# Masked cross-attention in a two-block transformer kernel: a new order of loads in SP's queue, reciprocals of 16 sums instead of 256 columns, masks made by VectorE, and a third buffer of last products

## The reference, cut to what matters

```
q = split_heads(layernorm(x) @ Wq + bq)          # 16 heads of 16
k = split_heads(ctx @ Wk + bk)                   # 257 keys per sequence
v = split_heads(ctx @ Wv + bv)
scores = einsum('bhqd,bhkd->bhqk', q, k) / 4
scores = where(mask[:, None] > 0, -1e9, scores)  # mask: 128 x 32 x 257, int32
p = softmax(scores)
x = x + einsum('bhqk,bhkd->bhqd', p, v) @ Wo + bo
```

## Time and profile before

| | |
|---|---|
| median of 3 runs | 3450.29 us (3443.96 to 3454.62) |
| profiled execution, its own time | 3441.18 us |
| its span in the profile | 3439.3 us |
| mean granted TensorE clock over the span | 0.879 |
| busy over the span | PE 78%, DVE 63%, ACT 54%, POOL 51% |
| HBM traffic over the span | 45 GB/s |

### The profile page before, as it was taken

The page is one execution under the profiler, slowest core; times in us unless marked ns, Lnnn a source line. Parts: engine busy times, 40 slices in busy tenths (PEclk is TensorE's granted clock), DMA queues, the critical chain, the costliest instruction groups (busy, mean ns, idle before and its releaser), DMA issues. The chain is left out here.

```text
span 3439.3 us, 83459 instructions
## 1 busy us (share of the span) xinstructions
PE 2694.3 (78%) x32206; PEld 2065.0 (60%) x32206; DVE 2159.9 (63%) x4574; ACT 1851.9 (54%) x4252; POOL 1758.3 (51%) x1653
## 2 busy tenths in 40 slices
PE   4766777677776775999975969999999488743998
PEld 3555566555555563555543558888887366642776
DVE  4556665566655664777774367777777588673443
ACT  3445554455544556777742457777777366533333
POOL 4455544554445535777761056666665477505332
PEclk9888888888888896998887989999999699956999
DMA  3211122111221100000000021121110000053110
GB/s 117 74 51 50 50 61 64 50 50 50 59 66 50 50 26 18 1 1 1 1 1 26 1 87 57 57 69 59 57 57 30 15 2 2 7 205 131 39 39 28
DMA packets 120961, 160.19 MB, mean 47 GB/s; under 512 B 11456, under 2 KB 107840, under 8 KB 118400
## 3 DMA queue, kind: packets, MB, share of 16 engines
q1 hardware_dynamic: 115904, 140.28, 14.0%
q0 software_dynamic: 4672, 14.57, 1.2%
HBM read 139.99 MB, written 14.83 MB: 45 GB/s over the span
## 5 line engine op out<-in xcount | busy, mean ns | idle before, releaser
L579 ACT ACTIVATE x_prob<-x_prob,x_nm 128x257 f32<-128x257 f32 x512 | 254.3, 498 | 536.6 <-DVE x_nm L666 536.6
L666 DVE CUSTOM_DVE_ANT_0 x_prob<-x_psS,x_masked,x_lastv 128x256 f32<-128x256 f32 x512 | 216.1, 476 | 313.2 <-POOL x_prob L342 313.2
L1901 DVE TENSOR_TENSOR_SCAN m_s<-m_a,m_psD 128x1024 f32<-128x1024 f32 x128 | 284.9, 2267 | 1.3 <-PE m_psD L1728 1.3
L484 PE MATMUL x_psS<-x_kh,x_qbdh 64*128 64x256 f16 x512 | 79.9, 304 | 215.5 <-DVE x_nm L666 215.5
L673 DVE SCALAR_TENSOR_TENSOR x_pTl<-x_psT,x_pTh 128x1024 f16<-128x1024 f32 x128 | 156.6, 1223 | 146.6 <-ACT x_pTh L586 146.6
L1202 DVE SCALAR_TENSOR_TENSOR x_pTl<-x_psS,x_pTh 128x1024 f16<-128x1024 f32 x128 | 156.7, 1224 | 145.4 <-ACT x_pTh L1110 145.4
L315 POOL TENSOR_SCALAR x_ctxh<-x_ctx 128x512 f16<-128x512 f32 x128 | 78.9, 616 | 326.8 <-DMA x_ctx<-in_ctxT 326.8
L394 PE MATMUL x_psK<-x_ctxh,x_wkh 128*128 128x256 f16 x512 | 157.8, 308 | 103.3 <-DVE x_kl L680 100.6
L1840 ACT ACTIVATE m_a<-m_dt,m_rate 128x248 f32<-128x248 f32 x512 | 206.8, 492 | 0.0
L349 POOL TENSOR_TENSOR x_pv<-x_vxr,x_prob 128x256 f32<-128x256 f32 x128 | 79.3, 620 | 214.8 <-PE x_psO L518 214.8
L1612 POOL TENSOR_TENSOR m_s<-m_s 128x1024 f32<-128x1024 f32 x64 | 150.4, 2350 | 66.8 <-DVE m_s L1901 66.8
(11 more groups left out here) (596 smaller groups left out, 11504.8 us busy)
## 6 DMA issues: line engine op xcount, KB each, us to landing
x_ctx<-in_ctxT SPq DMA_DIRECT2D x64, 1024.0 KB, 7.2
x_mraw<-in_mask SPq DMA_DIRECT2D x128, 128.5 KB, 4.4
x_vxr<-x_vx SPq DMA_DIRECT2D x32, 512.0 KB, 4.5
e1r_stage<-in_L_ffn_w SPq DMA_DIRECT2D x16, 1024.0 KB, 4.9
e_rows<-e1r_pad POOLq DMA_DIRECT2D x1, 5070.0 KB, 20.7
e1t_row<-e_rows SPq DMA_DIRECT2D x39, 130.0 KB, 2.1
all_xres<-in_x SPq DMA_DIRECT2D x1, 4096.0 KB, 14.1
x_vxr<-x_vx SPq DMA_DIRECT2D x128, 32.0 KB, 3.5
```

The source lines that it names most:

```text
L579: last = act.activation(prob[b % NP][:, s, :], prob[b % NP][:, s, :], ACT.Exp, bias=nm[b % NP][:, s:s + 1], scale=-1.0, accum_out=sm[b // ...
L666: dve.tensor_tensor_reduce(prob[b % NP][:, s, 0:LAST], psS[:, s * LAST:(s + 1) * LAST], masked[g % 2][:, j, :], -SC, lastv[g % 2][:, j, s: ...
L1901: dve.tensor_tensor_scan(states, rates, psD[at % 2][:], 0.0, ALU.mult, ALU.add).then_inc(scan_done, 1)
```

## The change

Four things are changed together. SP's loop issues the context of group g+1 first, then the masks of g, then the last values of g; the context of group 1 is still loaded ahead of the loop. `to_add` moves from POOL to DVE: once ahead of the loop, and then in slot j=0 after the residual; the waits for `s_min` and `last_done` that guarded its buffers on POOL go, since DVE itself is the reader. DVE takes the reciprocals of the 16 sums per partition (`shares`, in place in `sm`, slot j=0, after the minima) ahead of their spreading, so that `spread_sums` on POOL waits for DVE (`share_done`) instead of ACT, PE's matmul yields the reciprocal denominators directly, and `normalise` only multiplies, reading them from PSUM; PE's last_scores wait for `o_norm` instead of `share_done`. The products of the last values get three buffers instead of two, and value_last waits for one attend fewer.

```diff
--- before.py
+++ after.py
@@ -215,10 +215,10 @@
         nm = [sb(f"nm{n}", [P, 4], F32) for n in range(NP)]
         sm = [sb(f"sm{n}", [P, GB, 4], F32) for n in range(2)]
         pT = parts("pT", [P, 2, 512], NW)
-        pv32 = [sb(f"pv32_{n}", [P, D], F32) for n in range(2)]
+        pv32 = [sb(f"pv32_{n}", [P, D], F32) for n in range(3)]
         sums = sb("sums", [P, 4, GB, T], F32)
         oT = [sb(f"oT{n}", [P, C, GB, T], F32) for n in range(2)]
-        shares, ob = sb("shares", [P, D], F32), sb("ob", [P, C, P], F32)
+        ob = sb("ob", [P, C, P], F32)
         (obp,) = parts("ob", [P, C, P], 1)
         vx_dram = nc.dram_tensor("x0_vx", (NB, D), F32, kind="Internal").ap()
 
@@ -297,12 +297,12 @@
             sync.wait_ge(vx_done, 1)
             sync.dma_start(vx_dram, vx32[:]).then_inc(vx_out, 16)
             sync.wait_ge(vx_out, 16)
-            for g in range(NT):
+            load_vx(0)
+            for g in range(1, NT):
+                if g + 1 < NT:
+                    load(g + 1)
+                load_mask(g)
                 load_vx(g)
-                if g > 0:
-                    load_mask(g)
-                if g > 1:
-                    load(g)
 
         @block.gpsimd
         def _(pool):
@@ -328,13 +328,6 @@
                         con["mask4h"][:].unsqueeze(1).unsqueeze(3).to_broadcast([P, C * GB, 4, T]), ALU.mult)\
                         .then_inc(qbd_ready, 1)
 
-            def to_add(g):
-                pool.wait_ge(mask_in, 64 * (g + 1))
-                wait(pool, s_min, 4 * GB * (g - 1))
-                wait(pool, last_done, g - 1)
-                pool.tensor_scalar(mlast[g % 2][:], mraw[:, :, LAST], 0.0, BIG * SC, ALU.is_gt, ALU.mult)
-                pool.tensor_scalar(masked[g % 2][:], mraw[:, :, 0:LAST], 0.0, -BIG, ALU.is_gt, ALU.mult).then_inc(mask_done, 1)
-
             def place_last(b):
                 pool.wait_ge(last_done, b // GB + 1)
                 wait(pool, t_mm, b - NP + 1)
@@ -345,14 +338,14 @@
                 g, j = b // GB, b % GB
                 pool.wait_ge(exp_done, b + 1)
                 pool.wait_ge(vxr_in[g % 2], 16 * (g // 2 + 1))
-                wait(pool, pv_mm, b - 1)
-                pool.tensor_tensor(pv32[b % 2][:].rearrange("p (c r n) -> p c r n", c=C, r=RG),
+                wait(pool, pv_mm, b - 2)
+                pool.tensor_tensor(pv32[b % 3][:].rearrange("p (c r n) -> p c r n", c=C, r=RG),
                                    vxr[g % 2][:, j, :].rearrange("p (c r n) -> p c r n", c=C, r=RG),
                                    strips(prob[b % NP][:, :, LAST]).unsqueeze(3).to_broadcast([P, C, RG, 64]), ALU.mult)\
                     .then_inc(pv_last, 1)
 
             def spread_sums(g):
-                pool.wait_ge(exp_done, (g + 1) * GB)
+                pool.wait_ge(share_done, g + 1)
                 wait(pool, sum_mm, g)
                 pool.tensor_tensor(sums[:], eye_q[:].unsqueeze(1).unsqueeze(1).to_broadcast([P, 4, GB, T]),
                                    sm[g % 2][:].rearrange("p j s -> p s j").unsqueeze(3).to_broadcast([P, 4, GB, T]),
@@ -368,7 +361,6 @@
             pool.wait_ge(const_in, 112)
             for b in range(2):
                 split(b)
-            to_add(0)
             spread(0)
             for b in range(2, GB):
                 split(b)
@@ -381,7 +373,6 @@
                 batch(split, b + GB)
                 if j == 0:
                     group(spread_sums, g - 1)
-                    group(to_add, g + 1)
                 if j == 1:
                     group(add_bo, g)
                 batch(place_last, b + 1)
@@ -433,7 +424,7 @@
 
             def last_scores(g):
                 pe.wait_ge(qbd_ready, 2 * (g + 1))
-                wait(pe, share_done, g - 1)
+                wait(pe, o_norm, g - 1)
                 if g == 0:
                     pe.wait_ge(kx_lo, 1)
                 for j in range(GB):
@@ -516,7 +507,7 @@
                     to = (c * 2 + b % 2) * P
                     for r in range(RG):
                         last = pe.matmul(psO[64 * r:64 * r + 64, to:to + P],
-                                         pv32[b % 2][:, c * P + 64 * r:c * P + 64 * r + 64], con["ident"][:],
+                                         pv32[b % 3][:, c * P + 64 * r:c * P + 64 * r + 64], con["ident"][:],
                                          start=False, stop=True, skip_group_check=True)
                 last.then_inc(pv_mm, 1)
 
@@ -653,7 +644,6 @@
                 dve.wait_ge(sx_mm, g + 1)
                 dve.wait_ge(mask_done, g + 1)
                 wait(dve, placed, (g - 1) * GB)
-                wait(dve, s_min, 4 * GB * (g - 1))
                 dve.scalar_tensor_tensor(lastv[g % 2][:], psX.rearrange("p (j s) -> p j s", j=GB), -SC,
                                          mlast[g % 2][:].unsqueeze(2).to_broadcast([P, GB, 4]),
                                          ALU.mult, ALU.add).then_inc(last_done, 1)
@@ -696,10 +686,17 @@
             def normalise(g):
                 dve.wait_ge(sum_mm, g + 1)
                 dve.wait_ge(o_ext, 2 * g + 2)
-                dve.reciprocal(shares[:], psA).then_inc(share_done, 1)
-                dve.wait_ge(share_done, g + 1)
                 row = oT[g % 2][:].rearrange("p c j t -> p (c j t)")
-                dve.tensor_tensor(row, row, shares[:], ALU.mult).then_inc(o_norm, 1)
+                dve.tensor_tensor(row, row, psA, ALU.mult).then_inc(o_norm, 1)
+
+            def shares(g):
+                dve.wait_ge(exp_done, (g + 1) * GB)
+                dve.reciprocal(sm[g % 2][:], sm[g % 2][:]).then_inc(share_done, 1)
+
+            def to_add(g):
+                dve.wait_ge(mask_in, 64 * (g + 1))
+                dve.tensor_scalar(mlast[g % 2][:], mraw[:, :, LAST], 0.0, BIG * SC, ALU.is_gt, ALU.mult)
+                dve.tensor_scalar(masked[g % 2][:], mraw[:, :, 0:LAST], 0.0, -BIG, ALU.is_gt, ALU.mult).then_inc(mask_done, 1)
 
             def lo_ob(g):
                 dve.wait_ge(ob_ready, g + 1)
@@ -731,6 +728,7 @@
             lo_k(0)
             lo_q(0)
             lo_k(1)
+            to_add(0)
             last_values(0)
             for b in SLOTS:
                 g, j = b // GB, b % GB
@@ -739,7 +737,9 @@
                 if b % 2 == 0 and 0 <= b - 4 < NB:
                     extract((b - 4) // 2)
                 if j == 0:
+                    group(shares, g - 1)
                     group(residual, g - 2)
+                    group(to_add, g + 1)
                 if j == 2:
                     group(normalise, g - 1)
                 if j == 3:
```

## The result

The changed kernel takes 3101.73 us (median of 4 runs, 3098.22 to 3103.22) against 3447.73 before (4 runs): a ratio of 0.8993, 95% interval 0.8975 to 0.901, 346 us less. Forecast were 3135 us and a range of 3075 to 3210. The profiled execution took 3103.2 us, 338 less than that of before; the layer itself ended at 947.2 instead of 1290.8 us, 343.6 earlier, and the rest of the program took 5.7 us more in this execution. That is scatter: over all fourteen traces of this case the rest, which none of them changes, took 2145.6 to 2155.1 us, and it took 5.4 us less in a second trace of the changed kernel itself. So where two medians lie less than some 10 us apart, I read the layer's end and the length of a group instead.

A forecast was written before the change was run, and what follows sets the result against it. Masked cross-attention was taken as bounded by waits for the late context, once a group. At -10.65 us per group (stall -10.3, reciprocal -1.6, masks +1.25), plus start and end, -315 us gave 3135 us; range 3075 to 3210.

The forecast's parts named there:

- The late context: VectorE's minima wait, through GpSimd, for the context's DMA; SP's new order removes this stall, 10.3 us per group.
- Masks on VectorE: Slot j=0: masks take about 0.75 us on VectorE, and the slot grows by 1.25 us including a held tensor_scalar.
- the hold: Slot j=0: GpSimd's spread of sums locks out VectorE's small mask tensor_scalar; without it, 0.8 us per group better.
- Reciprocals: Slot j=2: loses the 1.76 us reciprocal of 256 columns and its wait for TensorE, 1.6 us back.
- Third buffer: Removes GpSimd's waits for TensorE, 161.2 us in 1000, no time by themselves, but SP asks for the masks earlier.
- the masks' margin: Slot j=0: masks behind the context land after 8.7 us, wanted after 9.9 us: just in time, margin 1.2 us.
- The sum: Per group: stall -10.3, reciprocal -1.6, masks +1.25, so -10.65 us; -315 us in all, with start and end.
- Rival A: TensorE binds the masked cross-attention: period falls to 26.6 us, 12.2 less per group, 3089 us; chance 0.10.
- Rival B: Masks land 1 to 4 us after VectorE wants them, behind the context: 3165 to 3255 us; chance 0.20.
- C: Rival: holds between VectorE and GpSimd spread to two more slots, 2.4 us each group, 3207 us; chance 0.05.
- Rival D: Slower than before: mask loads over 10.5 us late stop VectorE; at 22 us after SP's release, 3498 us; chance 0.02.
- E: Rival: SP still caught at the last values, context stays late; only 5.2 us per group gained, 3293 us; chance 0.03.

The follow-up runs named there:

- the kernel with the wide reciprocal: The changed kernel with the reciprocal of 256 columns in PSUM again and the spread of sums released by ACT: 3122.16 us, ratio 0.9071.
- the later kernels at 26.14 us: The changed kernel with VectorE's masks in slot j=1 and the token normalisation (L174) moved in front of L663 there: 3055.09 us, ratio 0.8881.

## Why the prediction was right, point by point

1. **The late context was the stall, and the order its cure**: shown. Slot 0 to 1 lost 10.41 us (forecast 10.3), and the order alone gives 292 of 346 us. That the parts overlap was missing from the sum's reasoning but not from its number, since there the stall was counted once. (The 11.0 us that the prediction calls the context's flight run from SP's release; the context itself was issued at 630.44 and flew 8.6 of them.)

2. **Masks on VectorE**: the mechanism was right, the size a bit high: slot 3 to 0 grew by 0.90 us, forecast 1.25. The duration was 0.68 instead of 0.75; the hold was 0.8 us, as forecast. The 0.75 was a loose reading: the two rows, 0.16 us at 2 elements and 0.181 at 32, give 0.7 ns an element as they stand, which is 0.88 us at 1024, and with a row rounded to 0.01 us they could not fix it closer. The upper bound of 1.22 us, an operation reading PSUM, did not apply. The Trainium skill (VectorE: DVE Perf Modes, "What auto-detection actually checks") has an enabled instruction take its two-port double mode if its single source and its destination are in SBUF with outermost sizes even or equal; 0.68 us for 1024 elements a partition against 1.22 for L663, which reads PSUM, agrees with it. The Trainium skill's rule of the hold (SBUF — State Buffer, "Who interferes with whom") was borne out in both directions by the 0.98 and 0.73 us above, and by 0.16 us as soon as POOL's spread no longer ran beside it.

3. **Reciprocals**: this is the term that was mis-sized. The step was "1.6 us back". The slot lost 1.98. I had a row for the full clock's return but gave it no price, and I read the 5.31 us (614.29 to 619.60) as the reciprocal's alone, while TensorE, for which VectorE waited there, ran at half its clock until 617 us:

```profile
615.00:616.00 1.00, 1.00 (x6) 0.68 (x5) 1.00 (x7) 1.00 (x5) 1.00 (x1) 0.50 0.00 0
617.00:618.00 1.00, 1.00 (x10) 0.65 (x7) 0.55 (x2) 0.00 (x0) 0.92 (x2) 1.00 0.00 0
```

In all 29 groups of before the clock over this slot was 0.54 to 0.66. Sorted by the clock, the kernels show what the reciprocals are worth. At a clock of 1.00 the slot takes 7.16 us with the narrow form and 8.33 to 8.40 with the wide one, 1.2 us apart (the order alone has four groups at 8.62 to 8.68 as well). At 0.80 it takes 8.41 to 8.79 us with the narrow form (all but the order, masks on POOL) and 8.56 to 8.86 with the wide one (order only): next to nothing apart. So the two causes cannot be added. From 9.14 us, the full clock with the wide form gives 0.74 (8.40, the kernel with the wide reciprocal), the narrow form without the order only 0.21 (8.93), and both together 1.98. The 1.6 us came true only because the order brought the clock back; that the number is close is partly luck. The 0.4 us above it is the choice of the sample: in that group the slot took 8.67 us (610.93 to 619.60), in the mean 9.14.

4. **Third buffer**: wrong in its words. Alone it is worth 87 us, in the changed kernel 17. And the masks' margin, 1.2 us by my proportion, was near zero: 13 short waits in 30 groups, of which the hold hid all but three. Part of the missing margin is plain in the traces: SP needed 2.27 us for the four mask loads instead of 1.86, and they landed 6.0 us after their issue (median) instead of 4.4.

5. **The sum**: -11.5 us a group instead of -10.65, 25 us in 30 groups. The start cost 6.8 us (forecast 6), the end gave 2.4 (forecast 1.5); with 3 us in the first and last groups that is the 343.6 us of the layer. Against the profiled execution, -315 were forecast and -338 measured. The other 8 us between the medians are scatter: the profiled execution of before was 6.6 us faster than its median, that of the changed kernel 1.5 us slower.

Rival A did not come: the period stayed over 27, and the later kernels at 26.14 us show that TensorE was not the limit. Rival B came in its mildest form. Of C, one half came and cost nothing: POOL's copy was held by VectorE's masks for 0.5 us, but VectorE waited for that copy only once in the layer (3.3 us). Rival D was far, E was excluded, and its price was wrong.

What stays open: the masks' loads land after 6.0 us behind the context and after 2.7 us when they go out apart from it, but whether memory or the queue makes the difference was not tried; and what decides whether TensorE's clock falls after the same idle stretch.

## What to carry to other kernels

Find the load that is issued when it is wanted, and look at what stands ahead of it in the issuing queue: a wait that belongs to another buffer can delay it by a whole period. Then price every other change by where it stands in the chain that is left: the same masks took 3.6 us on one engine, cost 0.9 ahead of an operation that was ready, and next to nothing in a slot that waits anyway. Where a stall is long enough to halve TensorE's clock, removing it returns more than its length, and a new short wait can cost nearly twice its own. A saving on another engine may not show until that clock is back, so sort the groups by clock before a mean is split into causes. And where two waits stand side by side, removing one alone shows only the other.

## What the runs showed of the hardware that I had not expected

A wait of 1.7 us on VectorE, which gave TensorE an idle stretch of 2.5 us between two thin windows (0.91 and 0.57 of 2 us busy), was followed by a clock of 0.50 in 14 of 29 groups and not in the other 15, although the program and the idle stretch are the same in each. The narrow reciprocals saved 1.2 us of a slot at a clock of 1.00 and next to nothing at 0.80. Of the 0.8 us that POOL held VectorE's tensor_scalar, only 0.58 came back when the hold was removed. Four mask loads landed 6.0 us after their issue behind a load of 1 MB and 2.7 us without it.
